# Distances as two products of the full array, placed one sub-convolution later, with the hidden-state gates ahead of the gathers

## What is computed

```python
h = jnp.maximum(_layernorm(x, axis=-1), 0.0)          # h is "x" below
...
h = _bn(_conv1d(xc, conv1_w, 0), ...); h = relu(h)
h = _bn(_conv1d(h, conv2_w, 8), ...)                  # 17 taps
x_conv = transpose(relu(h + xc))
s = x @ w_se.T + b_se                                 # 3 numbers a node
sq = jnp.sum(s * s, axis=-1)
dist = sq[:, :, None] + sq[:, None, :] - 2.0 * einsum('bnd,bmd->bnm', s, s)
A = jnp.exp(-dist) * mask
msg = jax.nn.relu(x @ w_msg.T + b_msg)
x_nmp = jnp.einsum('bnm,bmd->bnd', A, msg)
x_in = concatenate([x_conv, x_nmp]);  gi = x_in @ w_ih.T + b_ih;  gh = x @ w_hh.T + b_hh
r = sigmoid(gi_r + gh_r);  z = sigmoid(gi_z + gh_z);  n = tanh(gi_n + r * gh_n)
out = x + (1.0 - z) * n + z * h
```

## Time and profile before

| | before |
|---|---|
| median of 3 runs | 283.03 us (282.77 to 283.75) |
| the profiled execution | 282.48 us, its span in the profile 280.7 us |
| granted TensorE clock | 0.998 of 2.4 GHz |
| TensorE busy | 273.1 us (97% of the span) |
| VectorE busy | 244.4 us (87%) |
| ScalarE / GpSimd busy | 162.0 / 63.3 us |

### The profile page before, as it was taken

One profiled execution on the slowest core, in us unless ns is written; L12 is line 12 of the kernel. 1 busy time (PEld: TensorE's weight loads), 2 busy tenths in 40 slices (PEclk: granted clock), 3 DMA queues, 4 the chain that ended last, 5 costly groups with the idle time before them and its releaser, 6 DMA issues.

```text
span 280.7 us, 5274 instructions
## 1 busy us (share of the span) xinstructions
PE 273.1 (97%) x1842; PEld 246.4 (88%) x1842; DVE 244.4 (87%) x550; ACT 162.0 (58%) x270; POOL 63.3 (23%) x125
## 2 busy tenths in 40 slices
PE   7899999999999999999999999999999999999993
PEld 6699977999889988899889998899889998899883
DVE  6899988998999999988999989988999887984656
ACT  3798558737654657526754467536674267542463
POOL 7600020920225002610216002530116100340000
PEclk9999999999999999999999999999999999999999
DMA  7830405656243654182542743263440712043002
GB/s 229 304 43 0 147 6 154 223 117 183 77 152 56 149 198 138 42 132 81 218 152 39 166 152 112 113 95 112 152 152 7 124 54 96 2 61 70 0 0 75
DMA packets 20029, 30.77 MB, mean 110 GB/s; under 512 B 9458, under 2 KB 13876, under 8 KB 19124
## 3 DMA queue, kind: packets, MB, share of 16 engines
q1 hardware_dynamic: 17312, 26.50, 28.6%
q0 software_dynamic: 2544, 3.93, 10.2%
q10 hardware_dynamic: 148, 0.01, 0.0%
HBM read 25.41 MB, written 8.70 MB: 122 GB/s over the span
## 4 chain that ended last, share of the span: by engine, by line
PE 87%; DVE 5%; DMA 2%; ACT 2%; issue 1%; POOL 1%; SPq 0%; DVEq 0%; ACTq 0%; POOLq 0%
PE ps L1311 24%; PE ps L1313 23%; PE ps L1312 23%; PE ps L1364 5%; PE ps L1401 4%; DMA w<-w_conv 2%; PE ps L1424 2%; PE ps L1430 1%; PE ps L1433 1%; PE ps L1391 1%; ACT cp L544 1%; POOL rstd L408 1%; DVE stats L827 1%; DVE n_lo L1031 0%; PE ps L1360 0%
## 5 line engine op out<-in xcount | busy, mean ns | idle before, releaser
L1311 PE MATMUL ps<-v_hi,wt_hi 128*128 128x256 f32 x280 | 79.3, 283 | 0.0
L1313 PE MATMUL ps<-v_hi,wt_lo 128*128 128x256 f32 x280 | 78.8, 282 | 0.0
L1312 PE MATMUL ps<-v_lo,wt_hi 128*128 128x256 f32 x280 | 78.7, 281 | 0.0
L1311 PEld LDWEIGHTS ps<-v_hi,wt_hi 128*128 128x128 f32 x280 | 52.7, 188 | 0.8
L1312 PEld LDWEIGHTS ps<-v_lo,wt_hi 128*128 128x128 f32 x280 | 52.6, 188 | 0.3
L1313 PEld LDWEIGHTS ps<-v_hi,wt_lo 128*128 128x128 f32 x280 | 52.7, 188 | 0.0
L581 ACT ACTIVATE mbs<-ps,par 128x256 f32<-128x256 f32 x24 | 12.0, 501 | 30.7 <-DVE y L970 17.6
L414 POOL TENSOR_TENSOR scale<-vpe,neg_half 128x8 f32<-128x8 f32 x6 | 10.2, 1695 | 83.3 <-DVE scale L844 83.3
L1311 PE MATMUL ps<-h_hi,wt_hi 128*128 128x512 f32 (+1 forms) x67 | 26.7, 398 | 0.5 <-DVE h_lo L879 0.3
L1312 PE MATMUL ps<-h_lo,wt_hi 128*128 128x512 f32 (+1 forms) x67 | 25.7, 384 | 0.0
L1313 PE MATMUL ps<-h_hi,wt_lo 128*128 128x512 f32 (+1 forms) x67 | 25.7, 384 | 0.0
(11 more groups left out here) (167 smaller groups left out, 642.3 us busy)
## 6 DMA issues: line engine op xcount, KB each, us to landing
w<-ln_rows SPq DMA_DIRECT2D x6, 1024.0 KB, 4.7
mask<-adj_t SPq DMA_DIRECT2D x8, 512.0 KB, 3.5
out<-x_t SPq DMA_DIRECT2D x7, 512.0 KB, 5.4
out<-gate POOLq DMA_DIRECT2D x14, 256.0 KB, 4.1
xin<-x_nm SPq DMA_DIRECT2D x6, 512.0 KB, 3.7
xt<-x_t SPq DMA_DIRECT2D x6, 512.0 KB, 4.3
slot_rows<-turned SPq DMA_DIRECT2D x24, 32.0 KB, 3.2
rows<-slot_rows SPq DMA_DIRECT2D x6, 128.0 KB, 3.0
```

What stands on the lines that cost most here:

```text
L1311: pe.matmul(dst, wt_hi[:, blk, :], hi, start=start, stop=False)
L1312: pe.matmul(dst, wt_hi[:, blk, :], lo, start=False, stop=False)
L1313: return pe.matmul(dst, wt_lo[:, blk, :], hi, start=False, stop=stop)
```

## The change

In groups 2 to 7 the right factors lie in a new tile `right_rows` of 128 rows and 2 x 512 columns, which GpSimd sets to zero once; four small DMAs put the factors of graph i of each four at rows 32 i to 32 i + 15 and columns 128 i to 128 i + 127. One product of 128 rows by 512 columns then gives the distances of four graphs, and there are two of them, into banks 5 and 7. The exponential is now two instructions, one a bank. The distances stand one sub-convolution later. `gates_h(g, 0)` stands ahead of the two gathers, and waits for the previous group's gate reads of banks 3, 4 and 6. On VectorE the two `join_y` of sub-convolutions 7 and 8 stand ahead of the two `masked`. To make room, `row_raw` and `row_hi` lie in `hg` and `right_rows`, and ScalarE waits for GpSimd's row_split before it first writes hg.

```diff
 # SP, factor_loads
-                upto(sp, rows_landed, 32 * done)
+                upto(sp, rows_landed, 80 * done)
...
                 sp.wait_ge(dist_ps, g)
+                sp.wait_ge(zeros_set, 1)
+                for i in range(4):
+                    first = SLOT * i
+                    sp.dma_start(right_rows[first:first + KD, :, i * P:(i + 1) * P].bitcast(F32),
+                                 slot_rows[first + KD:first + 2 * KD]).then_inc(rows_landed, 16)
                 sp.dma_start(rows[:, 0:4:2, :].bitcast(F32), slot_rows).then_inc(rows_landed, 16)
-                sp.dma_start(rows[0:P - KD, 1:4:2, :].bitcast(F32), slot_rows[KD:P]).then_inc(rows_landed, 16)
 # POOL, start
             pool.wait_ge(row_split, 3)
+            pool.memset(right_rows[:].bitcast(F32), 0.0).then_inc(zeros_set, 1)
 # ACT, exponent
+                if g > BY_TRANSPOSE:
+                    for q in range(2):
+                        act.activation(aff[:, 4 * q:4 * q + 4, :], bank(5 + 2 * q).rearrange("p (i n) -> p i n", n=P),
+                                       ACT.Exp, scale=2.0).then_inc(e_ready, 1)
+                    return
 # ACT, start
+            act.wait_ge(row_split, 3)
             by_graphs(0, 0, 6)
 # DVE, groups 2 to 7
                     add_shared(g, 1)
+                    join_y(g, 1, 0)
+                    join_y(g, 1, 1)
                     masked(g, 0)
                     masked(g, 1)
-                    join_y(g, 1, 0)
-                    join_y(g, 1, 1)
 # PE, distance
+                if g > BY_TRANSPOSE:
+                    pe.wait_ge(rows_landed, 80 * (g - BY_TRANSPOSE))
+
+                    pe.wait_ge(v_ready, NCH * g)
+                    pe.wait_ge(n_lo_ready, NCH * g)
+                    for q in range(2):
+                        last = pe.matmul(bank(5 + 2 * q), rows[:, 2 * q, :], right_rows[:, q, :], start=True, stop=True)
+                    last.then_inc(dist_ps, 1)
+                    return
 # PE, gates_h
-                if c == 0:
-
-                    pe.wait_ge(e_ready, g + 1)
+                if c == 0 and g > BY_TRANSPOSE:
+
+                    pe.wait_ge(ghn_ready, NCH * g)
+                    pe.wait_ge(r_ready, NCH * g)
+                    pe.wait_ge(z_ready, NCH * g)
 # PE, order of a group
-                else:
+                sub_conv(g, 7)
+                if g > BY_TRANSPOSE:
                     distance(g)
-                sub_conv(g, 7)
                 sub_conv(g, 8)
+                gates_h(g, 0, ahead)
                 if g > BY_TRANSPOSE:
                     gather(g, 0, 5)
                     gather(g, 1, 7)
-                gates_h(g, 0, ahead)
```

More of the change, by code:

```diff
@@ L74, in gnn_kernel @@
         neg_half = sb("neg_half", [P, GB])
-        row_raw = sb("row_raw", [33, 3 * MW])
-        row_hi = sb("row_hi", [33, 3 * MW], F32R)
+        right_rows = sb("right_rows", [P, 2, CW], F32R)
+        row_hi = right_rows[0:33, 1, 0:3 * MW]
         row = sb("row", [P, 3 * MW], F32R)
@@ L98, in gnn_kernel @@
         hg = sb("hg", [P, GB, P])
+        row_raw = hg[0:33].rearrange("p b n -> p (b n)")[:, 0:3 * MW]
         cp = sb("cp", [P, CPAD, GB])
@@ L118, in gnn_kernel @@
         rows = sb("rows", [P, 4, P], F32R)
-        msg = sb("msg", [P, 9, P])
+        msg = sb("msg", [P, GB, P])
         mask = sb("mask", [P, GB, P])
@@ L183, in gnn_kernel @@
         turned_ready, turned_stored, rows_landed = sem("turned_ready"), sem("turned_stored"), sem("rows_landed")
+        zeros_set = sem("zeros_set")
         slot_hi, slot_lo, slot_sq = sem("slot_hi"), sem("slot_lo"), sem("slot_sq")
@@ L637, in exponent @@
                 upto(act, nmp_ps, NCH * g)
+                if g > BY_TRANSPOSE:
[3 more added lines that the diff above has]
+                    return
                 act.activation(aff[:].rearrange("p (q i) n -> p i q n", i=4),
                                ps[:, 3:7, 0:2 * P].rearrange("p i (q n) -> p i q n", n=P), ACT.Exp,
-                               scale=2.0).then_inc(e_ready, 1)
+                               scale=2.0).then_inc(e_ready, 2)
             def n_high(g, c, src):
@@ L1021, in masked @@
             def masked(g, c):
-                dve.wait_ge(e_ready, g + 1)
+                dve.wait_ge(e_ready, 2 * g + c + 1)
                 dve.wait_ge(mask_landed, 16 * (g + 1))
@@ L1378, in distance @@
             def distance(g):
-                if g <= BY_TRANSPOSE:
-                    pe.wait_ge(rows_ready, g + 1)
-                else:
-                    pe.wait_ge(rows_landed, 32 * (g - BY_TRANSPOSE))
+                if g > BY_TRANSPOSE:
[6 more added lines that the diff above has]
+                    return
+                pe.wait_ge(rows_ready, g + 1)
                 if g == 0:
@@ L1465, in gates_h @@
                 h = (h_hi[g % 2][:, cols(c)], h_lo[g % 2][:, cols(c)])
-                if c == 0:
-                    pe.wait_ge(e_ready, g + 1)
+                if c == 0 and g > BY_TRANSPOSE:
+                    pe.wait_ge(ghn_ready, NCH * g)
+                    pe.wait_ge(r_ready, NCH * g)
+                    pe.wait_ge(z_ready, NCH * g)
+                elif c == 0:
+                    pe.wait_ge(e_ready, 2 * g + 2)
                     if g == 0:
```

## The result

| | before | after |
|---|---|---|
| median | 283.3 us (282.77 to 283.75, 4 runs) | 281.57 us (281.51 to 281.64, 4 runs) |
| ratio, 95% interval | | 0.9949 (0.9924 to 0.9974) |
| profiled execution | 282.48, span 280.7 | 281.62, span 279.8 |

Faster by 1.7 us, where 0.5 us was forecast, and 281.57 where 282.5 was. The forecast counted from 283.03, the median of three runs; a fourth run raised it to 283.3. Two things in this table ask for a reading. The two profiled executions are only 0.86 us apart, half of what the medians are; and the runs before lie 1 us apart, those after 0.13.

The account below looks back on a forecast made before the run. TensorE's own stream was taken to bound the kernel, VectorE second. Products -0.60 us and load waits +0.1 gave -0.5, so 283.03 - 0.5 = 282.5 us, range 281.9 to 284.3.

Parts of the forecast that it names:

- The products: Distances on TensorE: two 512-column products cost 0.46 us against 0.56 for the old eight, -0.10 in each of six groups.
- the three bounds: Cost of the new distance pair: 0.46 us from `gates_xc` spacing (taken), 0.64 from product spacing behind the gathers, 0.86 with gaps.
- the gaps stay: Rival, slower: the 0.4 us around the old eight products remains, 6 x 0.3 = +1.8 us, 284.8; chance 0.07.
- the products cost 0.32 each: Rival, no change: each 512-column distance product on TensorE takes 0.32 us, +0.5, 283.5; chance 0.06.
- The loads in the new place: Distance loads on SP's queue: most groups 0.2 to 1 us in hand, one or two may wait; 0.1 us in all.
- The late loads as a rival: Slower: five loads issued in a row land late for the distances; 283.9 to 286.4; chance 0.13.
- The covers: Work hiding what moved: `gates_h`, 2.1 us on TensorE, hides exponential and masks, by 0.8 and 1.0 us.
- the wait of 0.2 for n_lo: TensorE's wait at the second `gates_xc` product, placed in the last group; stays within 0.2 us either way.
- VectorE's stop: VectorE stands still about 1.0 us ahead of the second `join_y`, until `sub_conv(g, 8)` ends, in each group.
- the rival by which it reaches TensorE: Slower: VectorE's delay reaches TensorE through bank 5 or `xc_low`, 0.3 us in five groups, 283.9; chance 0.05.
- The step that failed: TensorE nowhere waits for the distances' loads in the old kernel; the runs' median stays 0.55 us above the profiled execution.
- Faster by more than 0.85 us: Rival, 282.0 or below: needs 0.14 or more a group, by overlapping products or a shorter start or end; chance 0.08.

Follow-up runs that it names:

- after_again: The new kernel, unchanged, timed again: 281.58 us, ratio 0.9954 to the kernel before.
- before_p4: A further profiled execution of the kernel before, unchanged: 282.33 us.
- order_only: The kernel before with its old products, loads and single exponential, but in the new order: 282.43 us, ratio 0.9987.
- two_more_loads: The new kernel with two further small loads into an unread tile ahead of the load of rows: 283.48 us, ratio 0.9997.
- rows_first: The new kernel with the large load of rows issued ahead of the four small ones: 281.54 us.
- full_only: The new kernel's products, loads and two exponentials, but in the order of the kernel before: 284.25 us, ratio 1.0047.
- Before_split: The kernel before with two of the four slot stores issued through ScalarE's queue instead of SP's: 282.38 us, ratio 0.9975.
- before_p3: A further profiled execution of the kernel before, unchanged: 283.89 us.

## Why the prediction was wrong

*The products.* Right in kind, a little small. The pair costs 0.45 and the eight 0.56: 0.11 a group, not 0.10. The pitch of a group (from one group's distances to the next one's) fell by more. Distances of groups 3 and 8 in the new kernel (after_again) and in an execution of before without such a wait (before_p4):

```profile
...
97.55 0.62 PE L1401 MATMUL ps<-right_rows,rows 128*128 128x512 f32 x2
...
258.48 0.62 PE L1401 MATMUL ps<-right_rows,rows 128*128 128x512 f32 x2
...
```

```profile
...
96.12 0.45 PE L1391 MATMUL ps<-rows 16*128 16x128 f32 x8
...
257.72 0.44 PE L1391 MATMUL ps<-rows 16*128 16x128 f32 x8
```

(258.48 - 97.55)/5 = 32.19 and (257.72 - 96.12)/5 = 32.32: 0.13 a group, 0.8 us in six, which is about the 0.75 between 282.33 and 281.58. Of the 0.02 beyond the products' 0.11 the order accounts for 0.01: order_only, with the old products, repeats after (259.12 - 97.58)/5 = 32.31. The last 0.01 a group is open. The value from the `gates_xc` spacing was the right one of the three bounds, and the rivals by which the gaps stay, or the products cost 0.32 each, are out.

*The loads in the new place.* Right in the result: the third group waits 0.1 in the trace in front and nothing in after_again, the others nothing, where 0.1 us in all was put. The sum for the fourth group was 1 us too late: `rows` is issued at 126.09 instead of 126.3 to 126.6 and takes 2.5 us, not 3.0. The late loads as a rival did not occur, but two_more_loads shows how near it was: its two further loads delay the issue of `rows` by 1.1 us in the fourth group, and that is enough.

*The covers.* Right: the 2.1 us of `gates_h` hide the masks with 0.8 to spare, and without them TensorE waits 7.1 us. One reading was wrong without harm: the wait of 0.2 for n_lo is not in the last group but at 35.88 us, in the first. VectorE's stop came out at 0.67, not 1.0. Its 0.3 us of lateness in the next group's first splits is there: they start at 138.22 in both traces, while the new one's TensorE is 0.3 ahead by then (0.16 at the distances, 129.78 for the 129.94 worked out, and 0.11 by their products). It costs nothing, so the rival by which it reaches TensorE did not occur. The change of the joins, which carries that, is worth nothing that could be measured.

*The step that failed* is in the first paragraph and in the sum: that TensorE "waits ... nowhere for the distances' loads", and with it "the median of the runs is 0.55 above that one", taken over as a constant. The first was read from one execution, in which that wait was absent. The 0.55 was the cost itself: in three of five profiled executions the kernel before waits 0.3 to 1.4 us in the sixth group, because the slots' last store lands late, and most of its timed runs lie above the floor: 12 of 24, 13 of 17 and 14 of 21 are above 282.6. The new kernel has no such excess (profile 281.62, median 281.57), so the 0.55 should not have been added to its time. Of the 0.93 us between 282.5 and 281.57 this is 0.55. The other 0.38 is nearly all the gain a group, 0.13 instead of 0.10 (0.2 in six), and the 0.15 that the profiled execution had over the floor at its start. Faster by more than 0.85 us was a rival, at 0.08, but neither of its conditions is what happened: the gain a group stayed below 0.14, and what lay beyond it was a wait in the middle that went away. I had worked out the microseconds in hand for the new place and never put the same question to the old one, though the trace had it. In the sixth group the stores of the slots already took 3.40, where those of the fourth took 2.66:

```profile
...
183.38 3.40 SPq L329 DMA_DIRECT2D slot_rows<-turned  x4
```

L334 left at 188.79, L335 0.6 later, at 189.4; landed after 3.2 that is 192.6, and TensorE wanted it at 193.2. That margin of 0.6 is smaller than what a landing varies by: from 2.4 to 3.3 for L334, and up to 4.0 for L335.

*What took the wait away* are two things, and the runs part them only roughly. The later place alone leaves 3 of 12 runs above 282.6 instead of 12 of 24 (order_only), which twelve runs don't tell clearly; rows_first shows it at work. And in all profiled executions with the new loads in which SP issues the four stores, it does so in 2.7 us in that group, though the last can still land late (rows_first, full_only). Before_split, which changes nothing but the queue of two stores, ends the scatter too, and two_more_loads brings one back, so the late arrival of these transfers is shown to be its cause. The highest profiled execution took 283.89 us; what the runs above that wait for, up to 286.0, was in no profile. Why the stores are slow in just that group is open. In 184 to 188 us before_p3 has two transfers of instructions, the new kernel (after_again) one (queue, number, MB, share):

```profile
...
q8 instruction: 1, 0.02, 1.4%
q14 instruction: 1, 0.01, 0.5%
...
```

```profile
...
q8 instruction: 1, 0.02, 1.6%
...
```

The other four executions of before have two as well, waiting or not, and so has order_only; before_split has one. That could fit stores whose issue is held up by transfers of instructions, which SP's three further DMAs a group would shift, though ScalarE's two stores in before_split are slow there with one. It says nothing of why the last store lands late in some executions only, and no run tried it by itself.

## What to carry to other kernels

A profile is one execution. Where the runs of a kernel scatter by more than the edit is worth, and the profiled one has the lowest time, ask first which wait isn't in it: look for transfers that land within a microsecond of their use, and take a second and a third profile. Compute the margin of each transfer in the old place as well as in the new one. And read short stalls from the steps between starts, since the view of waits leaves them out.

## What had not been expected of the hardware

A product pair that had to wait for its data costs 0.11 us more than the wait: 0.57 to the next product instead of 0.46 (third group of the new kernel, and every late group of two_more_loads). Its weight load starts with the product, both at 97.49, where in the fourth group it starts 0.12 us ahead (129.66 and 129.78). The eight small products in four row groups cost 0.56 us though they start within 0.2 us; the two of 128 rows cost 0.45 for eight times the rows: so in this stream, at this size, what the packing costs around it is more than it saves. And of 62 timed runs of the kernel before in three sets, the same program on the same inputs took from 282.25 to 286.0 us, while 12 runs of before_split stayed within 0.41 us and 10 of the new kernel within 0.2.
